# A state-space scan kernel: x and dt get separate buffers, loads and releases; tanh writes into the tile of the normed y

## The reference, cut to what matters

```python
xz = x @ W_in;  xh, z = split(xz)
xc = depthwise_conv_3x3(xh)                      # the "x" of the scan
dt_r, Bp, Cp = split(xc @ W_xproj)
dt  = softplus(dt_r @ W_dt + b_dt)
dtN = dt @ W_dtN + b_dtN
for t in range(48 * 48):                         # 2304 steps, one pixel of all images each
    h = exp(dt[t][:, :, None] * A) * h + (dtN[t] * Bp[t])[:, None, :] * xc[t][:, :, None]
    y = sum_n(h * Cp[t]) + Dskip * xc[t]
y = norm(y) * ln_g + ln_b
out = (y * silu(z)) @ W_out + b_out
```

## Time and profile before

| What | Value |
|---|---|
| Time, median of 3 runs | 4375.35 us (4368.41 to 4375.43) |
| Profiled execution: its own time / its span | 4363.87 us / 4362.1 us |
| DVE busy | 3931.4 us, 90% of the span |
| PE busy | 3367.6 us, 77% |
| POOL busy | 2815.9 us, 65% |
| ACT busy | 2803.7 us, 64% |
| PE clock granted, mean | 0.812 |
| DMA | 783.62 MB in the SP queue, its packets 78.0% of the 16 engines' time |

### The profile page before, as it was taken

One profiled execution on the slowest core, in us unless ns is written; L12 is line 12 of the kernel. 1 busy time (PEld: TensorE's weight loads), 2 busy tenths in 40 slices (PEclk: granted clock), 3 DMA queues, 4 the chain that ended last, 5 costly groups with the idle time before them and its releaser, 6 DMA issues.

```text
span 4362.1 us, 101858 instructions
## 1 busy us (share of the span) xinstructions
PE 3367.6 (77%) x33792; PEld 1637.9 (38%) x33792; DVE 3931.4 (90%) x13181; ACT 2803.7 (64%) x5762; POOL 2815.9 (65%) x5195
## 2 busy tenths in 40 slices
PE   5778787878787877777787878787878777777765
PEld 2334333433343334333343334333433343333322
DVE  2899999999999999999999999999999999999998
ACT  2666666666666666666666666666666666666654
POOL 0766666666666666666666666666666666666664
PEclk8778887888778878888888878887888788878776
DMA  3878788878888787878787878788888788787875
GB/s 73 201 184 191 182 187 184 189 184 186 184 192 184 186 187 183 190 180 194 181 193 179 190 183 192 178 188 185 189 186 185 181 188 188 182 189 180 187 165 116
DMA packets 300438, 790.14 MB, mean 181 GB/s; under 512 B 71301, under 2 KB 225926, under 8 KB 226182
## 3 DMA queue, kind: packets, MB, share of 16 engines
q1 hardware_dynamic: 299910, 783.62, 78.0%
HBM read 648.18 MB, written 96.73 MB: 171 GB/s over the span
## 4 chain that ended last, share of the span: by engine, by line
DVE 42%; PE 35%; ACT 11%; issue 6%; DMA 3%; SPq 2%; POOL 1%; ACTq 0%; POOLq 0%; DVEq 0%
PE ps_s L508 7%; DVE h L843 7%; PE ps_y L472 6%; DVE ps_a L827 6%; PE ps_s L563 5%; DVE h L846 5%; DVE ps_a L830 4%; ACT ps_a L618 4%; PE ps_y L456 3%; DMA xb<-xd 3%; DVE yn L915 3%; PE ps_s L517 3%; DVE dt L883 3%; PE ps_s L546 3%; PE ps_s L491 2%
## 5 line engine op out<-in xcount | busy, mean ns | idle before, releaser
L618 ACT ACTIVATE ps_a<-xb,a_n 128x384 f32<-128x384 f32 x2304 | 1247.0, 574 | 988.1 <-DVE h L846 973.5
L1150 POOL TENSOR_TENSOR mp<-ap,h 128x128 f32<-128x128 f32 x2304 | 1120.0, 486 | 544.6 <-ACT ap L628 407.9
L1160 POOL TENSOR_TENSOR h<-mp,up 128x128 f32<-128x128 f32 x2304 | 1090.6, 473 | 475.3 <-PE ps_y L472 293.0
L1140 POOL TENSOR_TENSOR up<-xb,db 128x512 f32<-128x512 f32 x576 | 627.5, 1089 | 486.3 <-DMA xb<-xd 408.5
L846 DVE SCALAR_TENSOR_TENSOR h<-xb,db,ps_a 128x192 f32<-128x192 f32 x2304 | 926.1, 402 | 0.0
L843 DVE SCALAR_TENSOR_TENSOR h<-xb,db,ps_a 128x192 f32<-128x192 f32 x2304 | 920.2, 399 | 2.2 <-PE ps_y L472 0.6
L472 PE MATMUL ps_y<-h,cw 64*32 64x256 f32 x18432 | 806.6, 470 | 93.5 <-DVE h L846 92.7
L827 DVE TENSOR_TENSOR ps_a<-ps_a,h 128x192 f32<-128x192 f32 x2304 | 810.3, 352 | 29.2 <-ACT ps_a L618 26.6
L830 DVE TENSOR_TENSOR ps_a<-ps_a,h 128x192 f32<-128x192 f32 x2304 | 805.6, 350 | 0.0
L628 ACT ACTIVATE ap<-xb,a_n 128x256 f32<-128x256 f32 x1152 | 519.1, 500 | 198.1 <-DMA xb<-xd 196.8
L472 PEld LDWEIGHTS ps_y<-h,cw 64*32 64x32 f32 x18432 | 319.7, 124 | 531.0 <-issue 322.3
(11 more groups left out here) (109 smaller groups left out, 4038.9 us busy)
## 6 DMA issues: line engine op xcount, KB each, us to landing
xb<-xd SPq DMA_DIRECT2D x576, 1024.0 KB, 7.9
xs<-xh SPq DMA_DIRECT2D x196, 192.0 KB, 8.6
xd<-dttok SPq DMA_DIRECT2D x288, 128.0 KB, 6.0
xin<-in_x_dram SPq DMA_DIRECT2D x144, 128.0 KB, 7.0
xd<-xtok SPq DMA_DIRECT2D x192, 96.0 KB
res<-in_x_dram SPq DMA_DIRECT2D x144, 128.0 KB, 7.1
out_dram<-res SPq DMA_DIRECT2D x144, 128.0 KB, 6.8
xd<-xtok SPq DMA_DIRECT2D x192, 64.0 KB
```

The lines of the kernel that those rows point to most:

```text
L618: ins = act.activation(ps_a[buf][:, n, 0:2 * VD].rearrange("p (t d) -> p t d", t=2), xb[:, u % XUNITS, 2 * buf:2 * buf + 2, 1, 0:VD], ACT.Exp,
L1140: pool.tensor_tensor(up[:, Q % 2], x4, db4.broadcast_to([P, 4, 2, VP]), ALU.mult).then_inc(u_ready, 1)
L1150: pool.tensor_tensor(mp[:, G % 2], ap[:, Q % 2, G % 4], h[:, (G - 1) % HRING, :, VD:HALF], ALU.mult) \
L1160: pool.tensor_tensor(h[:, G % HRING, :, VD:HALF], mp[:, G % 2], up[:, Q % 2, G % 4], ALU.add) \
```

## The change

x and dt go to separate halves of the DRAM tensor. There are two SBUF buffers: `xb` with four units of x alone, `dtb` with three units of dt alone, 3.5 MB in all as against 3 MB. Each unit now takes two loads of 512 KB on the same queue. The load of x of unit u waits for `h_ready` and `u_ready` of unit u-4. The load of dt of unit u waits for ACT's two semaphores of unit u-3, `a_ready` and `ap_ready`. At each s % 4 == 0 the queue gets first the dt of the unit two ahead, then the x of the unit three ahead. ACT waits for `dt_loaded`, DVE and POOL for `x_loaded`. `store_x` and `store_dt` each wait for the loads of their own kind. tanh goes into the first two slots of `yn` instead of `th`; `gate_tanh` then waits for `out_done` of the row before, and `scale_yn` for `sz_ready` of its own row. The numbers of DVE, PE and POOL instructions stay.

```diff
--- before.py
+++ after.py
@@ -28,7 +28,7 @@
 VD = 192
 VP = HALF - VD
 HRING = 8
-XUNITS = 3
+XUNITS, DUNITS = 4, 3
 XLN_ROWS = 4
 
 
@@ -119,7 +119,8 @@
         xtok = sb("xtok", [P, KT, DI])
         dttok = sb("dttok", [P, KT * DI])
 
-        xb = sb("xb", [P, XUNITS, 4, 2, HALF])
+        xb = sb("xb", [P, XUNITS, 4, HALF])
+        dtb = sb("dtb", [P, DUNITS, 4, HALF])
         h = sb("h", [P, HRING, 2, HALF])
         ap = sb("ap", [P, 2, 4, 2, VP])
         up = sb("up", [P, 2, 4, 2, VP])
@@ -133,7 +134,6 @@
         mvy = sb("mvy", [P, KT, 2])
         rsy = sb("rsy", [P, KT])
         yn = sb("yn", [P, NG, TOK])
-        th = sb("th", [P, 2, TOK])
         sz = sb("sz", [P, NG, TOK])
         res = sb("res", [P, KT, DM])
         st2 = sb("st2", [P, KT, 6])
@@ -160,7 +160,7 @@
         ps_s = [pb(f"ps_s{n}") for n in range(2)]
 
         bounce = nc.dram_tensor("bounce", [2, 2, IMAGES, NS, SIDE], F32, kind="Internal").ap()
-        xd = nc.dram_tensor("xd", [2, 2, IMAGES, SIDE, 2, HALF], F32, kind="Internal").ap()
+        xd = nc.dram_tensor("xd", [2, 2, 2, IMAGES, SIDE, HALF], F32, kind="Internal").ap()
 
         weights_in = sem("weights_in")
         taps_in = sem("taps_in")
@@ -214,6 +214,7 @@
         a_ready = sem("a_ready")
         ap_ready = sem("ap_ready")
         x_loaded = [sem(f"x_loaded{n}") for n in range(XUNITS)]
+        dt_loaded = [sem(f"dt_loaded{n}") for n in range(DUNITS)]
         m0_done = sem("m0_done")
         m1_done = sem("m1_done")
         h0_ready = sem("h0_ready")
@@ -345,33 +346,43 @@
                         sp.wait_ge(x_loaded[n], (r - 1) * (QUADS // XUNITS) * SEM_DMA)
                 for k, lo, n, j, q0 in X_PARTS:
                     for half in range(2):
-                        steps = xd[r % 2, half, :, :, 0, :].rearrange("b (q j) d -> j q b d", j=4)[j]
+                        steps = xd[r % 2, 0, half].rearrange("b (q j) d -> j q b d", j=4)[j]
                         sp.dma_start(steps[q0:q0 + n // IMAGES], xtok[lo:lo + n, k, half * HALF:(half + 1) * HALF]) \
                           .then_inc(x_stored, SEM_DMA)
 
             def store_dt(r):
                 sp.wait_ge(dttok_ready, r * KT + KT)
                 if r >= 2:
-                    for n in range(XUNITS):
-                        sp.wait_ge(x_loaded[n], (r - 1) * (QUADS // XUNITS) * SEM_DMA)
+                    for n in range(DUNITS):
+                        sp.wait_ge(dt_loaded[n], (r - 1) * (QUADS // DUNITS) * SEM_DMA)
                 for k in range(KT):
                     for half in range(2):
-                        sp.dma_start(xd[r % 2, half, :, 16 * k:16 * k + 16, 1, :].rearrange("b w d -> w b d"),
+                        sp.dma_start(xd[r % 2, 1, half, :, 16 * k:16 * k + 16, :].rearrange("b w d -> w b d"),
                                      dttok[:, k * DI + half * HALF:k * DI + (half + 1) * HALF]) \
                           .then_inc(dt_stored, SEM_DMA)
 
+            def spread(which, r, k):
+
+                src = xd[r % 2, which, :, :, 4 * k:4 * k + 4].rearrange("c b w d -> (c b) (w d)").unsqueeze(1)
+                return src.broadcast_to([2 * IMAGES, 8, 4 * HALF])
+
             def load_x(r, k):
-
                 u = r * QUADS + k
                 if k == 0:
                     sp.wait_ge(x_stored, (r + 1) * 2 * len(X_PARTS) * SEM_DMA)
-                    sp.wait_ge(dt_stored, (r + 1) * 2 * KT * SEM_DMA)
                 if u >= XUNITS:
                     sp.wait_ge(h_ready, 4 * (u - XUNITS + 1))
                     sp.wait_ge(u_ready, u - XUNITS + 1)
-                src = xd[r % 2, :, :, 4 * k:4 * k + 4].rearrange("c b w s d -> (c b) (w s d)").unsqueeze(1)
-                sp.dma_start(xb[:, u % XUNITS], src.broadcast_to([2 * IMAGES, 8, 4 * DI])) \
-                  .then_inc(x_loaded[u % XUNITS], SEM_DMA)
+                sp.dma_start(xb[:, u % XUNITS], spread(0, r, k)).then_inc(x_loaded[u % XUNITS], SEM_DMA)
+
+            def load_dt(r, k):
+                u = r * QUADS + k
+                if k == 0:
+                    sp.wait_ge(dt_stored, (r + 1) * 2 * KT * SEM_DMA)
+                if u >= DUNITS:
+                    sp.wait_ge(a_ready, 2 * (u - DUNITS + 1))
+                    sp.wait_ge(ap_ready, u - DUNITS + 1)
+                sp.dma_start(dtb[:, u % DUNITS], spread(1, r, k)).then_inc(dt_loaded[u % DUNITS], SEM_DMA)
 
             def bounce_states(r):
                 sp.wait_ge(db_ready, r + 1)
@@ -411,7 +422,12 @@
             for i in range(FIRST_ROW, LAST_ROW + 1):
                 for s in range(SIDE):
                     if s % 4 == 0:
-                        k = s // 4 + 2
+                        k = s // 4 + DUNITS - 1
+                        if k < QUADS and exists(i):
+                            load_dt(i, k)
+                        if k >= QUADS and exists(i + 1):
+                            load_dt(i + 1, k - QUADS)
+                        k = s // 4 + XUNITS - 1
                         if k < QUADS and exists(i):
                             load_x(i, k)
                         if k >= QUADS and exists(i + 1):
@@ -611,21 +627,21 @@
             def decay(pair):
                 u, buf = pair // 2, pair % 2
                 if u * 2 == pair:
-                    act.wait_ge(x_loaded[u % XUNITS], (u // XUNITS + 1) * SEM_DMA)
+                    act.wait_ge(dt_loaded[u % DUNITS], (u // DUNITS + 1) * SEM_DMA)
                 if pair >= 2:
                     act.wait_ge(h_ready, 2 * (pair - 1))
                 for n in range(2):
                     ins = act.activation(ps_a[buf][:, n, 0:2 * VD].rearrange("p (t d) -> p t d", t=2),
-                                         xb[:, u % XUNITS, 2 * buf:2 * buf + 2, 1, 0:VD], ACT.Exp,
+                                         dtb[:, u % DUNITS, 2 * buf:2 * buf + 2, 0:VD], ACT.Exp,
                                          scale=a_n[:, n:n + 1])
                 ins.then_inc(a_ready, 1)
 
             def decay_pool(Q):
-                act.wait_ge(x_loaded[Q % XUNITS], (Q // XUNITS + 1) * SEM_DMA)
+                act.wait_ge(dt_loaded[Q % DUNITS], (Q // DUNITS + 1) * SEM_DMA)
                 if Q >= 2:
                     act.wait_ge(hp_ready, 4 * (Q - 1))
                 for n in range(2):
-                    ins = act.activation(ap[:, Q % 2, :, n, :], xb[:, Q % XUNITS, :, 1, VD:HALF], ACT.Exp,
+                    ins = act.activation(ap[:, Q % 2, :, n, :], dtb[:, Q % DUNITS, :, VD:HALF], ACT.Exp,
                                          scale=a_n[:, n:n + 1])
                 ins.then_inc(ap_ready, 1)
 
@@ -730,6 +746,8 @@
 
             def scale_yn(r, g):
                 act.wait_ge(yt_done, r * NG + g + 1)
+                if g == 0:
+                    act.wait_ge(sz_ready, r * NG + NG)
                 if r >= 1 and g == 0:
                     act.wait_ge(out_done, r * KT)
                 act.activation(yn[:, g, :], shared_bank("yt", r, g)[:, 0:TOK], ACT.Identity, bias=bet[:, g:g + 1],
@@ -738,9 +756,11 @@
             def gate_tanh(r, g):
                 act.wait_ge(z_done, r * NG + g + 1)
                 n = r * NG + g
+                if r >= 1 and g == 0:
+                    act.wait_ge(out_done, r * KT)
                 if n >= 2:
                     act.wait_ge(sz_ready, n - 1)
-                act.activation(th[:, n % 2, :], shared_bank("z", r, g)[:, 0:TOK], ACT.Tanh, scale=0.5) \
+                act.activation(yn[:, n % 2, :], shared_bank("z", r, g)[:, 0:TOK], ACT.Tanh, scale=0.5) \
                    .then_inc(th_ready, 1)
 
             act.preload_act_table_set("natural_log_exp_and_others")
@@ -838,7 +858,7 @@
                     if u >= 2:
                         dve.wait_ge(c_done, u - 1)
                 a = ps_a[G // 2 % 2][:, :, G % 2 * VD:(G % 2 + 1) * VD]
-                x_t = xb[:, u % XUNITS, G % 4, 0, 0:VD]
+                x_t = xb[:, u % XUNITS, G % 4, 0:VD]
                 dve.wait_ge(m0_done, G + 1)
                 dve.scalar_tensor_tensor(h[:, G % HRING, 0, 0:VD], x_t, db[:, r % 2, 0, w:w + 1], a[:, 0],
                                          ALU.mult, ALU.add).then_inc(h0_ready, 1)
@@ -919,7 +939,7 @@
                 dve.wait_ge(th_ready, r * NG + g + 1)
                 if r >= 1 and g == 0:
                     dve.wait_ge(gated, r * NG)
-                dve.scalar_tensor_tensor(sz[:, g, :], th[:, (r * NG + g) % 2, :], 1.0,
+                dve.scalar_tensor_tensor(sz[:, g, :], yn[:, (r * NG + g) % 2, :], 1.0,
                                          shared_bank("z", r, g)[:, 0:TOK], ALU.add, ALU.mult).then_inc(sz_ready, 1)
 
             def add_residual(r, k):
@@ -1135,7 +1155,7 @@
                 pool.wait_ge(x_loaded[Q % XUNITS], (Q // XUNITS + 1) * SEM_DMA)
                 if Q >= 2:
                     pool.wait_ge(hp_ready, 4 * (Q - 1))
-                x4 = xb[:, Q % XUNITS, :, 0, VD:HALF].unsqueeze(2).broadcast_to([P, 4, 2, VP])
```

(1 more changed line is left out.)

## The result

The changed kernel takes **4393.54 us** (median of 5 runs, 4391.31 to 4394.05) against 4375.35 us before. The ratio over all runs of both kernels is 1.0045 with an interval of 1.003 to 1.006: slower by 0.45%, where 4368 us was forecast. The profiled execution has a span of 4389.5 us against 4362.1 us, 27.4 us more. Its median there was 4370.3 us for e1_pool8_late, e2_x_three_units, e3_tanh_alone and e5_cw_later, 4370.1 us for e6_pool10_late to e9_before_meeting and 4370.7 us for the last three.

What follows compares the result with a forecast made beforehand. DVE was taken as the bound, busy 3931.4 of 4362.1 us. Gains of 1.5, 2 and 4 us from earlier loads sum to 7.5 us, taking the 4375.35 us median to 4368 us; range 4326 to 4396 us.

Steps and rivals of the forecast that it cites:

- The sum of the loads: Gain from earlier dt loads at three places of the chain of waits: 7.5 us, bounds 1.5 and 19.1 us.
- the first row of the scan: Row without gate or output stages, where loads nearly set DVE's pace: 4 us gain taken, from nothing to 8.7 us.
- The other two places: Load waits at s = 7 and s = 35, five rows each: gains of 1.5 us and 2 us taken.
- ACT's 973.5 us of room: ACT's waits for DVE's h, 973.5 us, taken as room that absorbs earlier loads.
- those 700.9 us: POOL's waits for ACT's ap (407.9 us) and TensorE's ring (293.0 us), said to cover POOL's earlier start, valued at nothing.
- Rival B: POOL's L1140, starting earlier, stretches one more L957 or like (s = 40 to 42, or L910): 36 us slower; chance 0.15.
- A: ACT's load waits at s = 7 and s = 35 to 40 reach DVE every row: 48 us faster, 4327 us; chance 0.16.
- C: POOL's new phase leaves DVE's L957 alone: 45 us less, 4330 us; chance 0.11.
- D: Smaller loads cost DMA time: 4548 us, or 6682 us if loads set the time; chance 0.03.
- E: dt still lands late, queued behind x, so waits stay: within 0.2%; chance 0.03.
- The added 1.1 us behind `store_x`: On SP's queue, back-to-back stores and loads send the second dt load two issues, 1.1 us, later; cost nothing.
- The stores, the tanh, the strides: Store waits, ACT's tanh in yn with added waits, and half-stride reads in L843, L618, L628: each taken as zero.

Runs made afterwards that it cites:

- e1_pool8_late: Changed kernel plus one wait: POOL starts the ninth unit's L1160 only after DVE finishes step 28; 4364.03 us, ratio 0.9986.
- e2_x_three_units: Changed kernel with three units of x instead of four, x loaded and released at the old place; 4363.71 us, ratio 0.9980.
- e3_tanh_alone: Kernel before with only the tanh in the tile of the normed y and its two added waits; 4371.77 us, ratio 1.0002.
- e5_cw_later: Changed kernel with DVE's weigh_c of the third third moved from behind step 27 to behind step 29; 4363.45 us, ratio 0.9987.
- e6_pool10_late: e1_pool8_late with POOL also waiting for DVE's step 40 before its first L1170 of the eleventh unit; 4335.23 us, ratio 0.9921.
- e9_before_meeting: Kernel before with DVE's weigh_c of the last third moved from behind step 27 into step 30, onto POOL's L1140; 4380.11 us, ratio 1.0023.
- the last three: POOL waits (fourth unit behind step 10, eleventh behind step 40) in kernel before, e2_x_three_units and changed kernel: 4312.75, 4308.39, 4344.4 us.

## Why the prediction was wrong

**The sum of the loads came out in size.** 7.5 us were forecast for the earlier dt. The kernels with the split and without the meeting came to ratios of 0.9986, 0.9987 and 0.9980, that is 6 to 9 us of 4370. Of these the first row of the scan holds some 3 us where 4 were taken: it lasts 76.1 us before, 73.0 in e1_pool8_late and 73.5 in e2_x_three_units. The other two places were not measured apart. Two readings were a little off: the 1.5 us are what L531's matmuls wait for xp, and its weight loads wait another 8.3 us (14 times); and of the ten later pieces of the chain five are at s = 7, but four at s = 35 and one at s = 31. Neither changes the sum beyond its bounds. ACT's 973.5 us of room held.

**The step that failed** is the one at POOL: "I cost POOL's gain at nothing, covered by those 700.9 us." The waits cover POOL's own lateness, and they did. What they don't cover is that POOL's L1140, moved some 3 us earlier, stands where DVE runs L859, and that this alone makes the stretch behind step 27 0.88 us longer, 26 us net in the kernel (e1_pool8_late). The cost is not a wait in any list: it is a longer DVE instruction, so no view of waits shows it, neither before nor after.

**Rival B was the true mechanism, in another place.** It was priced at 36 us and given 0.15. It named L957 and L910. Those did not move: 712 and 650 ns before, 710 and 643 ns after. The instruction hit was L859 behind step 27, and so the sign of B that was named, DVE's busy time up in L957, L883, L915 or L910, did not come. B's test could have been made on the trace before. It says "it decides if POOL's start of a unit is set by the load there". Of POOL's units, the ninth waited longest for its load, 3.21 us in the row shown and 3.2 us in the mean; taking that wait away puts L1140 right behind POOL's last step, at DVE's step 27, and L859 with two SBUF inputs stands exactly there. The prediction checked the groups that were already long, and L859 was short (0.57 us for the pair) *because* the load was late.

**A** was wrong: ACT's waits for loads fell by 165.7 us, and in e1_pool8_late, where no meeting blurs it, DVE waits 116.9 us for rsy and 53.3 us for rs, no less than the 113.2 and 46.9 us before. **C**: POOL left L957 as it was; it took the added waits of e6_pool10_late to bring that to 409 ns. **D**: the DMA share went down, not up, and a 512 KB load lands in 5.2 us (x) or 6.1 us (dt), around the 5.8 us taken. **E**: the loads came early.

*SP.* The added 1.1 us behind `store_x` had no effect that a run shows. *The stores, the tanh, the strides*: nothing, and for the tanh tile e3_tanh_alone shows it. L863 and L866 keep 399 and 401 ns with the new stride.

The Trainium skill (SBUF — State Buffer, Who interferes with whom) says that a DVE instruction with two SBUF inputs contends with a GpSimd instruction that reads SBUF, over a port pair that is locked for a whole instruction, so that the other fully blocks. The trace agrees: 1140 ns for a 278 ns instruction behind a POOL one of 1.10 us, and no change in L863 and L866, each of which has only one tensor input in SBUF (399 ns with POOL idle, 400 ns with POOL busy throughout). The Trainium skill (DMA: Bandwidth & Descriptors, Bandwidth) advises batches of at least 1 MiB. This case shows no loss from going below: with loads in flight together, halves of 512 KB moved the same bytes at a lower DMA share.

## What to carry to other kernels

When an edit takes a wait away from an engine that has room, ask where its next long instruction will then stand, and which instructions of the critical engine stand there now; a wait can be what keeps two of them apart. Look above all at short ones with two SBUF inputs, and at groups whose shortest and longest record differ widely (L957: 397 and 1150 ns); a short one may be short only because nothing runs beside it. Where one engine has room, a cheap added wait that holds it off such stretches can be worth more than the removed one: here 1.4% against 0.2%. It has to be measured, since one such wait cost 16 us by itself, and where it paid, the chain through TensorE and ACT carried the gain.

## What the runs showed of the hardware

- One POOL instruction of 1.06 to 1.10 us over 512 elements stretches a DVE instruction of 0.28 us with two SBUF inputs to 1.14 us, and what that costs the kernel depends on the waits behind it: 26 us of 40 in one setting, 34 in another.
- DVE's L863 and L866, with one tensor input in SBUF, one in PSUM and a scalar in SBUF, take 399 ns with POOL idle and 400 ns beside it.
- Splitting 1024 KB loads (7.9 us to landing) into 512 KB ones (5.2 and 6.1 us) left the bytes as they were and the packets' share of DMA time went from 78.0 to 69.9%. Other transfers landed sooner: xs<-xh in 5.7 us, 8.6 before.
- The same added wait changed the time by +16 us in one kernel and by -25 us in another, with TensorE's mean clock at 0.803 and 0.823, and at 0.82 and 0.93 in steps 39 to 47. Why is open.
